# A macaron block on one core: separate chunk lists for its two expert stages, a new plan, and normalized rows from ScalarE

## What is computed

```python
x = x + 0.5 * ffn(layernorm(x))       # stage A
x = x + attn(layernorm(x))            # stage B
x = x + 0.5 * ffn(layernorm(x))       # stage C, the same weights as A

# attn: 8 heads of 32; q = x Wq^T, latent = x Wkv_down^T (64), k, v from latent
# softmax(q k^T / sqrt(32)) v, then Wo^T
# ffn: 8 experts, each token takes its two best
probs = softmax(x gate_w^T + gate_b)
vals, idx = top_k(probs, 2)
h = relu(x w1[e] + b1[e])             # 128 -> 256
y = h w2[e] + b2[e]                   # 256 -> 128
out = sum over the two chosen experts of vals * y
```

## Time and profile before

| | |
|---|---|
| median of 3 runs | 1413.15 us (1411.16 to 1414.05) |
| the profiled execution | 1422.18 us |
| its span, first to last instruction | 1420.4 us |
| mean granted clock of PE | 0.935 |
| instructions | 26803 |
| weight loads from DRAM (wt<-packed) | 338 of 320 KB |
| moved by DMA | 209.58 MB, 148 GB/s over the span |

### The profile page before, as it was taken

The page is one execution under the profiler, slowest core; times in us unless marked ns, Lnnn a source line. Parts: engine busy times, 40 slices in busy tenths (PEclk is TensorE's granted clock), DMA queues, the critical chain, the costliest instruction groups (busy, mean ns, idle before and its releaser), DMA issues.

```text
span 1420.4 us, 26803 instructions
## 1 busy us (share of the span) xinstructions
PE 1260.7 (89%) x8995; PEld 840.4 (59%) x8995; DVE 905.6 (64%) x2454; ACT 648.6 (46%) x1297; POOL 796.3 (56%) x783
## 2 busy tenths in 40 slices
PE   2888798898999998998989899999998999997793
PEld 1575476575656764665755466566654566573583
DVE  3764658678388965774786747777757655554232
ACT  0224444544554645454534464556454555463230
POOL 1023646636666557676546567666577546756533
PEclk9988899899999999998999899999898999998797
DMA  9206461674435864335731464545221473572841
GB/s 310 91 16 192 127 210 63 188 212 151 120 103 169 265 188 151 118 108 152 226 112 35 126 198 148 172 147 173 76 71 33 123 210 120 179 242 85 306 138 49
DMA packets 173643, 209.58 MB, mean 148 GB/s; under 512 B 17402, under 2 KB 116418, under 8 KB 173508
## 3 DMA queue, kind: packets, MB, share of 16 engines
q1 hardware_dynamic: 152672, 172.79, 39.7%
q0 software_dynamic: 15360, 31.49, 7.5%
q10 hardware_dynamic: 5476, 3.59, 0.8%
HBM read 159.04 MB, written 48.76 MB: 146 GB/s over the span
## 4 chain that ended last, share of the span: by engine, by line
PE 51%; DVE 16%; POOL 13%; issue 8%; DMA 7%; ACT 2%; ACTq 1%; SPq 0%; POOLq 0%; DVEq 0%
PE psum L1445 44%; POOL pairs L949 6%; DVE neg_m L1400 4%; POOL Y L1000 4%; DMA Y<-results_C,posC 3%; PE psum L1666 3%; POOL slots_C L980 3%; DVE X L1384 3%; DMA slots_C<-xnC,posC 2%; PE psum L1544 2%; PE psum L1508 1%; DMA Y<-results_A,posA 1%; POOL slots_A L980 1%; DVE neg_hl L1409 1%; PE psum L1609 1%
## 5 line engine op out<-in xcount | busy, mean ns | idle before, releaser
L1400 DVE TENSOR_REDUCE neg_m<-psum 128x1 f32<-128x512 f32 x512 | 317.2, 682 | 151.3 <-PE psum L1445 144.0
L949 POOL TENSOR_TENSOR pairs<-probs 128x512 f32<-128x512 f32 x256 | 321.1, 1278 | 123.0 <-ACT probs L1069 117.8
L1445 PE MATMUL psum<-nat 32*128 32x512 f32 x2048 | 365.1, 652 | 8.1 <-ACT m_rows L1078 2.8
L1069 ACT ACTIVATE probs<-psum 128x512 f32<-128x512 f32 x512 | 264.5, 610 | 101.2 <-PE psum L1445 90.4
L980 POOL DMA_INDIRECT slots_A<-xnA,posA x120 | 119.3, 994 | 192.3 <-DVE posA L1368 82.9
L1445 PEld LDWEIGHTS psum<-nat 32*128 32x128 f32 x2048 | 148.2, 189 | 116.2 <-issue 37.5
L1445 PEld LDWEIGHTS psum<-xg_T,wt 128*128 128x128 f32 x1352 | 173.0, 202 | 47.1 <-issue 28.8
L1445 PE MATMUL psum<-xg_T,wt 128*128 128x128 f32 x1352 | 189.5, 290 | 7.6 <-DMA wt<-packed 7.1
L1000 POOL DMA_INDIRECT Y<-results_C,posC x120 | 115.6, 963 | 122.7 <-DMA Y<-results_C,posC 95.4
L980 POOL DMA_INDIRECT slots_C<-xnC,posC x120 | 117.5, 979 | 99.4 <-DMA slots_C<-xnC,posC 48.8
L1445 PEld LDWEIGHTS psum<-wt,hg 128*128 128x128 f32 x1352 | 170.8, 198 | 3.6
(11 more groups left out here) (189 smaller groups left out, 1628.1 us busy)
## 6 DMA issues: line engine op xcount, KB each, us to landing
wt<-packed SPq DMA_DIRECT2D x338, 320.0 KB
xs<-slots_A SPq DMA_DIRECT2D x37, 256.0 KB
results_A<-ys SPq DMA_DIRECT2D x37, 256.0 KB
xs<-slots_C SPq DMA_DIRECT2D x37, 256.0 KB
results_C<-ys SPq DMA_DIRECT2D x37, 256.0 KB
X<-in_L_attn_x_dram SPq DMA_DIRECT2D x16, 256.0 KB, 5.8
out_dram<-X SPq DMA_DIRECT2D x16, 256.0 KB
packed<-probs SPq DMA_DIRECT2D x1, 2560.0 KB, 8.1
```

The source lines that it names most:

```text
L949: pool.tensor_tensor(pairs[:, kt // 2, j, :], probs[:, kt - 1, j, :], probs[:, kt, j, :], ALU.add).then_inc(S["p_added"], 1)
L1069: act.activation(probs[:, kt, j, :], at.banks()[j][:], ACT.Exp, scale=SCALE).then_inc(a_done, 1)
L1400: V_.tensor_reduce(neg_m[:, g, n, j:j + 1], at.banks()[j][:], AX.X, ALU.max, negate=True).then_inc(d_done, 1)
L1445: return nc.tensor.matmul(dst, w, m, start=start, stop=stop)
```

## The change

Four things change.

1. The stages get lists of their own, A_CHUNKS = (1,1,2,3,3,3,3) and C_CHUNKS = (3,3,3,3,2,1,1). Chunk numbers 0 to 6 are A's, 7 to 13 are C's. The first chunk of A and the last of C stay dense.
2. The constants of the planner's due times are all new, and several lengths in PARTS are longer.
3. The last part of scaled moves from DVE to ACT. DVE does the Newton step and, now for stage B too, shift = -mean * rstd (plus 1 in A and C); ACT computes rows * rstd + shift by four activations of 128x128, one for each tile of tokens. The wait for the scatters of old rows moves with it.
4. One check of assert_reuse (q and k after the scores of the batch before) is made for PE's queue only.

```diff
-CHUNKS = (1,1,2,3,3,3,2,1)
-FIRST = tuple(sum(CHUNKS[:c]) for c in range(len(CHUNKS)))
-CHUNK_OF = tuple(c for c, m in enumerate(CHUNKS) for _ in range(m))
+A_CHUNKS, C_CHUNKS = (1, 1, 2, 3, 3, 3, 3), (3, 3, 3, 3, 2, 1, 1)
+CHUNKS = A_CHUNKS + C_CHUNKS
+CHUNKS_OF = {"A": range(len(A_CHUNKS)), "C": range(len(A_CHUNKS), len(CHUNKS))}
+FIRST = tuple(sum(CHUNKS[CHUNKS_OF[s][0]:c]) for s in "AC" for c in CHUNKS_OF[s])
+CHUNK_OF = {s: tuple(c for c in CHUNKS_OF[s] for _ in range(CHUNKS[c])) for s in "AC"}
 DENSE = {"A": 0, "C": len(CHUNKS) - 1}
...
-PERIOD, FIRST_B = 37.27, 75.39
-WANTED = {"norm": 1.74, "scaled": -0.56, "xT": -17.17, ("q", 0): -71.19, ("k", 0): -158.18, ("v", 0): 30.19,
-          ("v", 1): 4.0, ("q", 1): 21.62, ("k", 1): -0.12, "wo": 79.07}
-GROUP_GAP, MAX_PACE, S_FIRST, S_PACE, PV, ADD, SUM = 19.97, -0.53, 7.25, 3.06, -1.46, 49.32, 6.11
-A_LEAD, A_PACE, A_ROUTE, A_NORMS = 28.7, 7.1, 70.95, 0.38
-C_NORM, C_ROUTE, C_FIRST, C_PACE, C_GATHER = 53.53, 10.71, 56.75, 6.55, 14.54
-LOAD_AHEAD, W_AHEAD = 89.62, -15.32
+PERIOD, FIRST_B = 37.1, 69.39
+WANTED = {"norm": -10.12, "scaled": -1.05, "xT": -18.51, ("q", 0): -69.62, ("k", 0): -104.58, ("v", 0): 33.14,
+          ("v", 1): 0.22, ("q", 1): 17.78, ("k", 1): 7.53, "wo": 69.27}
+GROUP_GAP, MAX_PACE, S_FIRST, S_PACE, PV, ADD, SUM = 16.85, -0.47, 6.42, 3.29, -1.04, 48.06, 7.28
+A_LEAD, A_PACE, A_ROUTE, A_NORMS = 25.07, 8.22, 70.15, 8.3
+C_NORM, C_ROUTE, C_FIRST, C_PACE, C_GATHER = 54.52, 11.03, 52.26, 12.66, 13.88
+LOAD_AHEAD, W_AHEAD = 131.75, -1.62
...
-    "norm": ((("DVE", 1.75), ("ACT", 0.45)), 0.0), "scaled": ((("DVE", 1.9),), 0.0),
+    "norm": ((("DVE", 2.0), ("ACT", 0.45)), 0.0), "scaled": ((("DVE", 1.0), ("ACT", 1.4)), 0.0),
...
-    "max": ((("PE", 0.87), ("DVE", 2.5)), 0.0), "msplit": ((("DVE", 0.3),), 0.0), "mrow": ((("PE", 0.45), ("ACT", 0.48)), 0.0),
-    "s": ((("PE", 1.1), ("ACT", 1.95)), 0.0), "pv": ((("PE", 3.7), ("ACT", 0.48)), 0.0), "add": ((("POOL", 1.27),), 0.0),
+    "max": ((("PE", 1.02), ("DVE", 2.5)), 0.0), "msplit": ((("DVE", 0.6),), 0.0), "mrow": ((("PE", 0.45), ("ACT", 0.48)), 0.0),
+    "s": ((("PE", 1.28), ("ACT", 1.95)), 0.0), "pv": ((("PE", 3.7), ("ACT", 0.48)), 0.0), "add": ((("POOL", 1.27),), 0.0),
...
-    "top1": ((("DVE", 1.9), ("ACT", 0.25)), 0.0), "top2": ((("DVE", 1.7), ("ACT", 0.2)), 0.0),
+    "top1": ((("DVE", 2.2), ("ACT", 0.25)), 0.0), "top2": ((("DVE", 2.0), ("ACT", 0.2)), 0.0),
...
-    "rank2": ((("PE", 1.0), ("DVE", 4.5)), 0.0), "scat": ((("POOL", 2.5),), 3.0),
+    "rank2": ((("PE", 1.0), ("DVE", 5.2)), 0.0), "scat": ((("POOL", 2.5),), 3.0),
...
-    "gat": ((("POOL", 2.5),), 3.0), "comb": ((("DVE", 2.4),), 0.0), "store": ((("SP", 0.48),), 2.5),
+    "gat": ((("POOL", 2.5),), 3.0), "comb": ((("DVE", 3.5),), 0.0), "store": ((("SP", 0.48),), 2.5),
...
             for name in "qk":
-                later(now(name, g), then("s", g * TILES + TILES - 1))
+                later(now(name, g), then("s", g * TILES + TILES - 1), engines=("PE",))
...
@@ ACT @@
             def norm(at):
                 act.wait_ge(S["mv_done"], at.count("mv_done"))
+                wait(act, S["xn_done"], at.count("xn_done", "scaled", index=at.index - 1))
                 chain(act.activation(rstd[at.stage][:], veps[at.stage][:], ACT.Ln))
                 act.activation(rstd[at.stage][:], rstd[at.stage][:], ACT.Exp, scale=-0.5).then_inc(S["rstd_done"], 1)
+
+            def scaled(at):
+
+                s, b = at.stage, at.index
+                act.wait_ge(S["shift_done"], at.count("shift_done"))
+                if s != "B" and b >= XN_RING:
+                    old = b - XN_RING
+                    if CHUNK_OF[s][old] == DENSE[s]:
+                        act.wait_ge(a_full, at.count("a_full", "xTf", index=old))
+                    else:
+                        act.wait_ge(scat_in[s][old % XN_RING], scattered(s, old))
+                if s == "B":
+                    wait(act, d_full, at.count("d_full", "xT", index=b - 1))
+                for n in range(TILES):
+                    last = act.activation(xn[s][:, xn_place(s, b) + n, :], X[:, b % X_RING, n, :], ACT.Identity,
+                                          bias=shift[s][:, n:n + 1], scale=rstd[s][:, n:n + 1])
+                last.then_inc(S["xn_done"], 1)
...
@@ DVE, scaled, after the Newton step @@
-                if at.stage != "B" and at.index >= XN_RING:
-                    old = at.index - XN_RING
-                    if CHUNK_OF[old] == DENSE[at.stage]:
-                        dve.wait_ge(a_full, at.count("a_full", "xTf", index=old))
-                    else:
-                        dve.wait_ge(scat_in[at.stage][old % XN_RING], scattered(at.stage, old))
-                if at.stage == "B":
-                    for n in range(TILES):
-                        last = V_.tensor_scalar(xn["B"][:, n, :], xb[:, n, :], mv["B"][:, n, 0:1], r[:, n:n + 1],
-                                                ALU.subtract, ALU.mult)
-                else:
-                    plus = shift[at.stage]
-                    chain(V_.tensor_tensor(plus[:], mv[at.stage][:, :, 0], r[:], ALU.mult))
-                    chain(V_.tensor_scalar(plus[:], plus[:], -1.0, 1.0, ALU.mult, ALU.add))
-                    for n in range(TILES):
-                        last = V_.tensor_scalar(xn[at.stage][:, xn_place(at.stage, at.index) + n, :], xb[:, n, :], r[:, n:n + 1],
-                                                plus[:, n:n + 1], ALU.mult, ALU.add)
-                last.then_inc(S["xn_done"], 1)
+                plus = shift[at.stage]
+                wait(dve, S["xn_done"], at.count("xn_done", index=at.index - 1))
+                chain(V_.tensor_tensor(plus[:], mv[at.stage][:, :, 0], r[:], ALU.mult))
+                V_.tensor_scalar(plus[:], plus[:], -1.0, 0.0 if at.stage == "B" else 1.0, ALU.mult, ALU.add).then_inc(S["shift_done"], 1)
```

More of the change, by code:

```diff
@@ L211, in first_part @@
         after(key, *others, part=0)
-    for b in range(sum(CHUNKS)):
+    for b in range(sum(A_CHUNKS)):
         def now(name, k=0):
@@ L268, in all_steps @@
     for s in "AC":
-        for b in range(sum(CHUNKS)):
-            c = CHUNK_OF[b]
+        for b in range(sum(A_CHUNKS)):
+            c = CHUNK_OF[s][b]
             if s == "A":
@@ L511, in assert_reuse, with later @@
     at = {engine: {step: n for n, step in enumerate(order[engine])} for engine in ENGINES}
-    def later(new, *old):
-        for engine in ENGINES:
+    def later(new, *old, engines=ENGINES):
+        for engine in engines:
             for step in old:
@@ L544, in assert_reuse @@
                 later(following, first)
-    for b in range(1, sum(CHUNKS)):
+    for b in range(1, sum(A_CHUNKS)):
         def now(name, k=0):
```

80 lines of the change are left out of this document (41 added, 39 removed).

## The result

The changed kernel takes 1349.31 us at the median (4 runs, 1348.15 to 1360.36), the kernel before 1413.6 beside it (4 runs, 1411.16 to 1418.61). The ratio is 0.9561 [0.9513, 0.9609]: 62 us less, 4.4%. The forecast was 1387 with a range of 1360 to 1422. The direction was right, the size was not: the gain is more than twice the one forecast and lies outside the range. An execution over 1.5% above the fastest of its kernel counts as slow and is left out of medians and ratios; that is one of e14 and one of e16.

What follows compares the result with a forecast made beforehand. PE bounds the kernel to 1336 us, GpSimd's row of pairs the end. 1422.2 -9.0 (tiles) +2 -26 (tail) +10 (early) -6 (VectorE) +1 +2 (ScalarE) = 1396.2, less 9.0 for profiling: 1387; range 1360 to 1422.

Steps and rivals of the forecast that it cites:

- two-part reading: Whole kernel: PE bounds 200 to 1336 us; at the end GpSimd's serial scatters and gathers set the time.
- row of pairs: GpSimd's 240 serial pairs of indirect DMAs, scatters and gathers: 5.0 us each, without rest from 1155.55 us.
- step 2: Tail behind the last wo: 58 us instead of 84, gain 26, closed by the dense batch; +2 before it.
- early hole: Near 393.79 us: stage C's first two batches, 16 pairs or 79 us, slide later; forecast 1428, chance 0.15.
- step 3: Early stretch: stage C waits for batch 2's attention, not batch 0's; +10 us taken, bounds 0 and +20.
- slower rival: Early stretch: stage C's delayed pairs find no slack, the tail's 26 us is lost; 1428 us, chance 0.15.
- ScalarE's queue: Rival: ScalarE's waits for shift and scatters hold exps, PE's 23 us of such waits double; 1409 us, chance 0.12.
- a sign against it: Whole kernel: PE waits for ScalarE above 40 us were to show the forecast wrong.
- step 5: Planner's new due times and lengths: reorder queues, issue nothing by themselves; 0 us taken, bounds -15 and +15.
- Step 4: Normalized rows moved to ScalarE: -6 us for VectorE's relief, +1 for the hop, +2 for ScalarE's queue.
- Step 1: Chunk lists: 14 tiles fewer, 18.1 us of PE; stage A's 9.0 us taken in full.

Runs made afterwards that it cites:

- e14: The order of e11 with the normalized rows made by VectorE instead of ScalarE: 1377.56 us, ratio 0.9713 to the kernel before.
- e16: The changed kernel's lists, lengths and rows, with due times from a second search in the planner alone: 1393.31 us, ratio 0.9829 to the kernel before.
- e6: The changed kernel's lists, lengths and rows, with due times from a first search in the planner alone: 1405.82 us, ratio 0.9923 to the kernel before.
- e1: The changed kernel, every queue in the same order, with the normalized rows made by VectorE again: 1363.95 us, ratio 0.9667 to the kernel before.
- e2: The kernel before, same order, each routed chunk's last padding tile neither loaded nor computed (324 tiles, not 338): 1409.58 us, ratio 0.9956.
- e7: The changed kernel, same order, with a waited-for 256-column GpSimd fill ahead of each of 240 pairs of indirect DMAs: 1398.86 us, ratio 0.9866 to the kernel before.
- e3: The changed kernel with the planner's old lengths; lists, due times and ScalarE's rows kept: 1384.65 us, ratio 0.9794 to the kernel before.
- e8: The changed kernel with attention's 16 due-time shifts moved at random by at most 1.0 us, first draw: 1373.32 us, ratio 0.9692 to the kernel before.
- e11: The changed kernel with attention's 16 due-time shifts moved at random by at most 1.0 us, second draw: 1367.64 us, ratio 0.9685 to the kernel before.
- e12: The changed kernel with attention's 16 due-time shifts moved at random by at most 1.0 us, third draw: 1372.21 us, ratio 0.9706 to the kernel before.
- e18: The changed kernel with the old lengths and another set of due times moved by at most 1 us: 1401.61 us, ratio 0.9886 to the kernel before.
- e5: The changed kernel with the old lists and due times searched anew in the planner: 1386.13 us, ratio 0.9783 to the kernel before.
- e15: The changed kernel with the old lists and due times from a second search in the planner: 1410.85 us, ratio 0.9978 to the kernel before.
- neighbours: Either kernel with attention's due-time shifts moved at random by at most 1.0 us: ratios 0.9692, 0.9685, 0.9706 (changed kernel) and 1.007, 1.0145 (kernel before).

## Why the forecast was right and wrong

**Right.** The two-part reading held: the row of pairs sets the end. It does so in after too, where step 2 had the dense batch close the tail. The dense batch's last additions are done 47.6 us behind the last wo, about as priced; VectorE's last combine then waits 11.3 us for the last gathers:

```profile
1337.68 2.34 DVE L1353 SCALAR_TENSOR_TENSOR X<-psum,givenC,X 128x128 f32<-128x128 f32 x8
1351.33 2.31 DVE L1394 SCALAR_TENSOR_TENSOR X<-Y,gateC,X 128x128 f32<-128x128 f32 x8 [11.30 <-DMA Y<-results_C,posC]
```

The early hole did not come. In the window from 200 to 400 us PE is busy 184.64 us against 181.94 in before, and batch 2's wo came earlier, not later:

```profile
364.36 0.68 DVE L1403 TENSOR_TENSOR X<-psum,X 128x512 f32<-128x512 f32 x1
```

It stood at 393.79 before. The row's steps of 8 us or more that begin between 200 and 500 us sum to 54 us, not over 100. So step 3's +10 was a loss that did not occur, and the slower rival falls with it. ScalarE's queue did not block: PE's largest waits for ScalarE and, for the size of it, for the adds (who, for whom; us, times, longest):

```profile
PE psum L1518 <- ACT xnA L1058: 16.9, 3, 15.1
PE psum L1676 <- POOL pairs L955: 9.6, 4, 2.9
PE psum L1455 <- ACT probs L1093: 6.7, 12, 1.6
PE psum L1518 <- ACT xnC L1058: 6.0, 4, 1.9
PE psum L1455 <- ACT hg L1119: 4.5, 9, 1.5
```

All of PE's waits for ScalarE sum to 44.7 us in thirteen groups, over the 40 that the forecast had set as a sign against it. That mark was badly set: 24.9 of it are waits for the rows themselves, 15.1 in one wait at the kernel's start, and they take the place of PE's waits for VectorE's rows (30.5 us in before, the longest 13.7). The waits that the rival meant, for exps and evictions, went from 23.3 to 19.8 us.

**Wrong: step 5, "issue nothing by themselves ... I take 0".** This is the step that failed. It was priced at 0 with ends of -15 and +15, taken as a share of PE's holes. Under after's due times the lengths make 31 us between the means of seven orders, and a random shift of due times by at most 1 us moves either kernel by 10 to 24. The plan decides when batch 11's attention ends (999 to 1003 against 1025 to 1051 us) and what stands between it and the last burst. PE's holes were the wrong resource to take the bound from: GpSimd's row lost 206 us in long steps, 54 more than in after. What the plan as a whole is worth between before and after was not isolated, since before's due times were made for other lists and lengths. That the new lengths gain only under due times chosen with them is likely (e6 and e16) and not shown; which of the lengths (rank2, comb, msplit or max) does it is open.

**Step 4, a term mis-sized.** Forecast -6 for VectorE and +3 for ScalarE; measured some -10 together, 4 to 15 by order. VectorE's busy time fell to 822.4 us, not 845: the move alone took 62.7 us off it (e1), where step 4 had 53 - 6 = 47. The groups that moved had stalled up to 3244 ns, and in these three orders their going let the burst begin 7 to 22 us earlier; a 7% share of the chain was the wrong measure for that. Whether it is the work or the stalls that counted isn't separated. On ScalarE the line through a 128x4 and a 128x512 activation was no upper bound: one of 128x128 takes 490 ns from start to end and, in a row of four, 0.414 us of busy time each (26.5 us per 64), 79.5 us for all 192 against the 58 forecast, which is why ScalarE is busy 712.1 and not 690 (the forecast's own terms, 648.6 + 58 - 10, give 697). The estimate from the Trainium skill (ScalarE: Activation LUTs, Rules for kernel authors), 78 us, agrees with the trace; the same page's advice to leave multiply and add to VectorE does not, by some 10 us, in this kernel. With the Trainium skill's other page (SBUF — State Buffer, Who interferes with whom) the trace agrees in so far as the rows' stalls are gone on ScalarE, which took 528 ns at most. GpSimd's own instructions did not get shorter by it: 795.4 us busy with the rows on ScalarE, 793.0 in e1.

**Step 1, a term too large.** 14 tiles less gave 14.5 us of PE and some 6 us of time (e2), where the sum had 9 from stage A and expected stage C's in the tail. The reading "PE is the bound up to 1336, so it is taken in full" was too simple for a stretch in which PE and the row of pairs take turns: e7 shows the other one of the two on the path. Of PE's 44.3 us, some 15 to 22 are this work (22 by the expert matmuls and the turning of xs, 414.2 us in after against 436.6). The granted clock was 0.948 of full speed in after's profile and 0.935 in before's, and the largest group of matmuls took 641 ns at the mean, 652 in before:

```profile
L1455 PE MATMUL psum<-nat 32*128 32x512 f32 x2048 | 349.3, 641 | 7.0 <-DVE neg_m L1410 3.0 <-DVE lgA L1289 2.0 <-ACT probs L1093 0.8
```

The remaining 20 to 30 us don't come from fewer instructions: with the same ones as after, PE is busy 1217 to 1247 us in the eight other orders (e3, e6, e8, e11, e12, e16 to e18). How much of that is the clock, and how much is matmuls that wait inside their busy time, the runs don't separate. The clock doesn't explain the gain by itself: after's executions outside the profile had 0.958 to 0.963 and before's 0.932 to 0.950, but e5 had 0.949 to 0.962 and took 1386 us. Within the kernel before, an execution at a clock 0.01 lower took about 9 us longer (67 executions); which of the two follows from the other is open.

**Step 2, roughly right and in the wrong place.** Behind the last wo are 66.1 us, where 58 were forecast and 84 stood before. But 19 gathers stand behind the last scatters, not 12 or fewer, so the row is as full as ever; 18 steps in 85.1 us, 4.7 each. In the orders with the new lists and lengths the tail is 63 to 70 us (76 with e7's fills), with the old lists and new lengths 77 and 80 (e5, e15), with the new lists and old lengths 90, 105 and 73. So in the orders that were run the short tail came with both. And a short tail is no gain by itself: the last wo of e5 and that of e3 are at 1308 and 1292, their medians 1.5 us apart. The sum that fits both kernels is the burst's start and 265 or 301 us behind it.

**The account.** From neighbours, 58 of the 62 us belong to the design with its plan, and some 4 to the difference between the two kernels' own luck. Of the 58, the rows are some 10 (measured in after's orders) and fewer tiles some 6 (measured in before's). The other 42 or so belong to the plan and to the lists' earlier release of (9,10,11). That is a remainder and not a measurement, and its parts aren't separated: the lengths make 31 us under after's due times, which may count a lost fit; the burst's cut gives the lists some 20 as an estimate; e5, e6, e15 and e16 leave the lists open within 20 us on both sides. No kernel that was run is faster than after.

## What to carry to other kernels

Where queues are written out by a planner, price the order as a term of its own, with bounds of some 2% of the time, and take those bounds by shifting the plan a little on both kernels before a gain is credited to an edit; an edit is measured with the order held fixed, in two or three orders. Treat lengths and due times as one thing: here the old lengths under due times that came with the new ones cost 31 us without one instruction more, and the new lengths under due times from a search in the planner alone gave only a part of the gain (e6, e16). Look for a serial row beside the busy shares: an engine at 59% set this kernel's end, and its long steps fell by 54 us where the kernel gained 62.

## What the runs showed of the hardware that was not expected

- An activation's time depends on more than its columns here: 128x4 0.205 us and 128x512 from PSUM 0.607, but 128x128 from SBUF to SBUF with a scale and a bias per partition 0.485 at the median. The line between the short and the long form gives 0.30 us for it, far too little.
- The 128x128 TENSOR_SCALAR on VectorE ran up to 3355 ns in before and 3193 in e1 beside 342 at the median; the same step on ScalarE took 528 ns at most in after. The stalls are not the rows' alone: with the rows gone from VectorE, its 128x4 instructions still ran up to 4616 ns beside 170.
- A GpSimd fill of 315 ns, waited for, ahead of each of 240 pairs raised the row's median step from 4.93 to 5.28 us. The 240 fills are 76 us of work, and the span grew by 35.
- PE's busy time for the same 8853 matmuls was 1216 to 1247 us, from one order of the queues to the next.
